# Cross-attention block: norm weights and biases multiplied into the next matrices, three-product values and projection in the first attention, new engine orders

## The reference, cut to what matters

```python
# layer 0
xn = layernorm(x, ln1_w, ln1_b); yn = layernorm(ctx, ln2_w, ln2_b)      # (v - mean) * rstd * w + b
q = xn @ Wq; k, v = split(yn @ Wkv)                                     # 16 heads of 16
x = x + softmax(q k^T / 4) v @ Wproj + bproj
x = x + gelu(layernorm(x, ln3_w, ln3_b) @ W1 + b1) @ W2 + b2            # 256 -> 1024 -> 256
# layer 1
q = rope(rmsnorm(x, norm_w) @ wq); k = rope(ctx @ wkv[k]); v = ctx @ wkv[v]
q, k = q / max(|q|, eps), k / max(|k|, eps)
x = x + softmax(4 q k^T) v @ wout
```

## Time and profile before

| | us |
|---|---|
| median of 3 runs | 366.83 (364.96 to 367.35) |
| the profiled execution, its time | 367.27 |
| its span, first to last instruction | 365.5 |
| PE busy | 357.3 |
| DVE busy | 279.1 |
| ACT busy | 252.7 |
| POOL busy | 193.5 |

### The profile page before, as it was taken

How to read it: one execution, slowest core, us unless ns; L and a number is a source line. 1 busy time by engine, 2 the same in 40 slices (tenths; PEclk the granted TensorE clock), 3 DMA queues, 4 the chain that set the end, 5 groups by cost and what they waited for, 6 DMA issues and landing times.

```text
span 365.5 us, 11432 instructions
## 1 busy us (share of the span) xinstructions
PE 357.3 (98%) x4510; PEld 324.4 (89%) x4510; DVE 279.1 (76%) x654; ACT 252.7 (69%) x490; POOL 193.5 (53%) x194
## 2 busy tenths in 40 slices
PE   8999999999999998999999999999999999999996
PEld 5988888898878887899999999999999999998885
DVE  3699989869598777767886777788877776868752
ACT  2267676676677575774578978976987779966662
POOL 2266433534835338304576458458466755477920
PEclk9999999999999999999999999999999999999999
DMA  7854001100000000000000000000200010000001
...
DMA packets 15724, 12.55 MB, mean 34 GB/s; under 512 B 3252, under 2 KB 15032, under 8 KB 15672
## 3 DMA queue, kind: packets, MB, share of 16 engines
...
## 4 chain that ended last, share of the span: by engine, by line
PE 90%; DVE 6%; issue 2%; ACT 1%; POOL 0%; DVEq 0%; POOLq 0%; ACTq 0%
PE banks_s L1166 12%; PE bank_qk L1046 10%; PE banks_s L1091 7%; PE bank_o L1178 7%; PE bank_y L1178 6%; PE bank_y L1230 4%; PE banks_s L1219 4%; PE bank_t L1126 4%; PE bank_qk L1068 3%; PE bank_y L1147 3%; PE bank_t L1046 3%; PE bank_qk L1072 3%; PE bank_o L1082 3%; DVE row_max L2153 3%; PE bank_o L1210 2%
## 5 line engine op out<-in xcount | busy, mean ns | idle before, releaser
L400 POOL TENSOR_TENSOR norm_inv<-norm_sq_min,minus_half 128x32 f32<-128x32 f32 x16 | 87.6, 5478 | 47.9 <-DVE norm_sq_min L2248 47.9
L354 POOL TENSOR_TENSOR masked<-qkT_r,halves_t 128x512 fp32r<-128x512 f32 x32 | 32.6, 1039 | 60.8 <-DVE qkT_r L2146 60.7
L2153 DVE TENSOR_REDUCE row_max<-banks_s 128x8 f32<-128x1024 f32 x32 | 37.6, 1216 | 2.9 <-PE banks_s L1091 2.5
L575 ACT ACTIVATE PT<-banks_s 128x1024 f32<-128x1024 f32 x32 | 31.1, 1022 | 10.0 <-PE banks_s L1115 9.7
L1166 PE MATMUL banks_s<-lnT_hi,W_hi 128*128 128x256 f32 x120 | 35.4, 295 | 0.0
L676 ACT ACTIVATE PT<-banks_s 128x1024 f32<-128x1024 f32 x32 | 31.5, 1024 | 5.5 <-PE banks_s L1219 5.2
L1166 PE MATMUL banks_s<-lnT_hi,W_lo 128*128 128x256 f32 x120 | 33.9, 282 | 0.0
L1166 PE MATMUL banks_s<-lnT_lo,W_hi 128*128 128x256 f32 x120 | 33.9, 282 | 0.0
L1091 PE MATMUL banks_s<-masked,qkT_r 32*128 32x256 f32 x768 | 31.5, 294 | 0.9 <-DVE row_max L2153 0.7
L1091 PEld LDWEIGHTS banks_s<-masked,qkT_r 32*128 32x128 f32 x768 | 25.0, 183 | 7.5 <-issue 4.7
L619 ACT ACTIVATE W_s<-banks_s,b_cols 128x256 f32<-128x256 f32 x60 | 25.0, 471 | 6.6 <-PE bank_y L1178 4.7
...
## 6 DMA issues: line engine op xcount, KB each, us to landing
...
```

The lines of the kernel that those rows point to most:

```text
L354: nc.gpsimd.tensor_tensor(masked[:, r, 1, :, half, :], qkT_r[:, r, 1, :, :].bitcast(fp32), ones, ALU.mult)\
L400: nc.gpsimd.tensor_tensor(norm_inv[:, j, :], norm_sq_min[:, j, :], minus_half[:, :], ALU.pow).then_inc(c_norm_inv, 1)
L575: nc.scalar.activation(PT[:, 2 * h:2 * h + 2, :], banks_s[:, 2 * h:2 * h + 2, :], ACT.Exp, scale=HD ** -0.5)\
L2153: v.tensor_reduce(row_max[:, 8 * h:8 * h + 8], banks_s[:, 2 * h:2 * h + 2, :].rearrange("p n (r k) -> p (n r) k", k=TOK), AX.X, ALU.max).t ...
```

## The change

1. **Norm weights go into the matrices.** `Wq` is multiplied by `ln1_w` (`query_weight`, ACT), the key half of `Wkv` by `ln2_w` (`keys_weight`, DVE), its value half on the way into high and low parts (`values_weight_hi`, ACT, and `values_weight_lo`, DVE), and `W1` by `ln3_w` in `w1_split`. The biases become products: `ln1_b` with `Wq` gives a column `q_bias`, which `queries_keys_hi` and `queries_keys_lo` add; `ln2_b` with `Wkv` gives a row that is stored in an unused row of the weights, against which `yn` has a column of ones; `ln3_b` with `W1` (`mlp_bias_mm`, 16 float32 products with one column each) is added to `b1`. `centre` and `scale` become `normalise`, one subtraction and multiplication for each input; `centre_b` and `scale_b` become `normalise_b`. The weights and biases arrive by six small DMAs on ACT's queue, one number to a partition, instead of four rows.
2. **`values_a` and `project_a` take the three-product form.** POOL makes the high and low part of the value input (`values_in`, a cast and a subtraction of 128x256), DVE the low part of the projection's input (`on_lo_a`). `queries_keys_hi` is now three ACT instructions instead of one, `queries_keys_lo` three DVE instructions instead of one.
3. **`WARM_LATE` and the two spreading products are gone,** and all engines have new lists. The fillers behind the first `queries_keys_a` are 87 before and 96 after.

A function `head_norms_root`, which would take the power by Newton steps on DVE, is added but never called, as `POWERS` is 16.

```diff
+            def values_in(t):
+                j = t % 2
+                pool.wait_ge(A["inT_ready"], t + 1)
+                wait(pool, A["v_mm"], t - 1)
+                nc.gpsimd.tensor_copy(v_in[:, j, 0, :, :], inT[:, j, 2:4, :]).then_inc(a_v_in_hi, 1)
+                pool.wait_ge(a_v_in_hi, t + 1)
+                nc.gpsimd.tensor_tensor(v_in[:, j, 1, :, :], inT[:, j, 2:4, :], v_in[:, j, 0, :, :].bitcast(fp32), ALU.subtract).then_inc(a_v_in_lo, 1)
...
+                for k in range(KT):
+                    nc.scalar.activation(wq_a[:, k, :], Wq_s[:, k, :], ACT.Copy, scale=ln_cols[:, 0, k:k + 1]).then_inc(wa_q, 1)
...
+            def query_bias():
+                act.wait_ge(q_bias_mm, 1)
+                nc.scalar.activation(q_bias[:, :], bank_qk[:, 0:KT], ACT.Copy).then_inc(q_bias_ready, 1)
+            def context_bias():
+                act.wait_ge(bias_mm, 1)
+                act.wait_ge(c_wkv_padded, 2)
+                nc.scalar.activation(wk_a[C2B:C2B + 1, 1, :], bank_o[C2B:C2B + 1, 0:C1], ACT.Copy).then_inc(k_bias_ready, 1)
+                nc.scalar.activation(wkv_r[C2B:C2B + 1, 0, 1, C1:], bank_o[C2B:C2B + 1, C1:], ACT.Copy).then_inc(v_bias_hi, 1)
+            def out_weight_hi():
+                act.wait_ge(w_out_loaded, 2 * LOADED)
+                nc.scalar.activation(wout_r[:, 0], Wproj_s[:, :, :], ACT.Copy).then_inc(wa_out_hi, 1)
...
                 wait(act, a_shifted, t - 2)
-                nc.scalar.activation(qkT_r[:, t % RING, 0, :, :], bank_qk[:, :].rearrange("p (a b) -> p a b", a=4), ACT.Copy)\
-                    .then_inc(a_qk_hi, 1)
+                for m in range(KT):
+                    nc.scalar.activation(qkT_r[:, r, 0, m, :], bank_qk[:, TOK * m:TOK * m + TOK], ACT.Identity, bias=q_bias[:, m:m + 1])\
+                        .then_inc(a_q_hi, 1)
+                nc.scalar.activation(qkT_r[:, r, 0, KT:, :], by_row(bank_qk[:, 2 * TOK:]), ACT.Copy).then_inc(a_k_hi, 1)
...
+            def query_bias_mm():
+                pe.wait_ge(w_q_loaded, LOADED)
+                for m in range(KT):
+                    for k in range(KT):
+                        last = mm(bank_qk[:, m:m + 1], Wq_s[:, k, 128 * m:128 * m + 128], ln_cols[:, 1, k:k + 1], start=k == 0, stop=k == KT - 1)
+                last.then_inc(q_bias_mm, 1)
+            def context_bias_mm():
+                pe.wait_ge(w_att_loaded, 2 * LOADED)
+                mm(bank_o[:, :], bias_2[:, 0, :], Wkv_s[:, 0, :], start=True, stop=False)
+                mm(bank_o[:, :], bias_2[0:C2B, 1, :], Wkv_s[0:C2B, 1, :], start=False, stop=True).then_inc(bias_mm, 1)
...
-                for k in range(2):
-                    last = mm(bank_o[:, 0:C1], inT[:, t % 2, 2 + k, :], Wkv_s[:, k, C1:], start=k == 0, stop=k == 1)
-                last.then_inc(A["v_mm"], 1)
+                    pe.wait_ge(wa_v_lo, 2)
+                    pe.wait_ge(v_bias_lo, 1)
+                pe.wait_ge(a_v_in_lo, t + 1)
+                split_mm(bank_o[:, 0:C1], v_in[:, t % 2, :, :, :], wkv_r[:, :, :, C1:]).then_inc(A["v_mm"], 1)
...
-                    pe.wait_ge(w_out_loaded, 2 * LOADED)
-                for k in range(KT):
-                    last = mm(bank_y[:, 0:C1], onT[:, k, :], Wproj_s[:, k, :], start=k == 0, stop=k == KT - 1)
-                last.then_inc(A["proj_mm"], 1)
+                    pe.wait_ge(wa_out_lo, 1)
+                pe.wait_ge(a_onT_lo, t + 1)
+                split_mm(bank_y[:, 0:C1], onT_r[:, :, :, :], wout_r[:, :, :, :]).then_inc(A["proj_mm"], 1)
+            def mlp_bias_mm():
+                pe.wait_ge(w1_loaded, LOADED)
+                pe.wait_ge(w_b1_loaded, 4 * LOADED)
+                for m in range(HM):
+                    for k in range(KT):
+                        last = mm(bank_y[:, m:m + 1], W1_s[:, k, 128 * m:128 * m + 128], ln3_cols[:, 1, k:k + 1], start=k == 0, stop=k == KT - 1)
+                last.then_inc(b1_mm, 1)
...
-            for n in range(WARM_EARLY):
+            for n in range(WARM):
                 nc.tensor.transpose(bank_s[n % 4][:, 0:128], ident[:, :], ident[:, :])
-            pe.wait_ge(ln_rows_loaded, 4 * LOADED)
-            pe.wait_ge(ones_ready, 1)
-            mm(bank_qk[:, :], one_row, row_1, start=True, stop=True)
-            mm(bank_o[:, 0:2 * C2], one_row, row_2, start=True, stop=True).then_inc(rows_spread, 1)
-            for n in range(WARM_LATE):
-                nc.tensor.transpose(bank_s[n % 4][:, 0:128], ident[:, :], ident[:, :])
+            pe.wait_ge(ln_rows_loaded, 6 * LOADED)
             pe.wait_ge(bank_zeroed, 1)
-            busy(4, bank_t)
+            busy(7, bank_t)
+            query_bias_mm()
             inputs_a(0)
-            busy(7, bank_o)
+            context_bias_mm()
+            busy(9, bank_y)
+            pe.wait_ge(q_bias_ready, 1)
             queries_keys_a(0)
             pe.wait_ge(A["inT_ready"], 1)
             inputs_a(1)
-            values_a(0)
...
+                    v.tensor_scalar(wk_a[0:r, k, :], Wkv_s[0:r, k, 0:C1], ln_cols[0:r, 2, k:k + 1], None, ALU.mult).then_inc(wa_k, 1)
...
+                v.tensor_scalar(w1_part(W1_hi, u), w1_part(W1_s, u), ln3_cols[:, 0, u % 2:u % 2 + 1], None, ALU.mult).then_inc(w1_hi_done, 1)
                 dve.wait_ge(w1_hi_done, u + 1)
-                v.tensor_tensor(w1_part(W1_lo, u), w1_part(W1_s, u), w1_part(W1_hi, u).bitcast(fp32), ALU.subtract)\
+                v.scalar_tensor_tensor(w1_part(W1_lo, u), w1_part(W1_s, u), ln3_cols[:, 0, u % 2:u % 2 + 1], w1_part(W1_hi, u).bitcast(fp32),
+                                       ALU.mult, ALU.subtract)\
                     .then_inc(w1_lo_done, 1)
...
+            def mlp_bias():
+                dve.wait_ge(b1_mm, 1)
+                v.tensor_tensor(b1_all[:, :], b1_cols[:, :], bank_y[:, 0:HM], ALU.add).then_inc(b1_ready, 1)
...
-            def centre(t):
+            def normalise(t):
...
+                    dve.wait_ge(a_padded, 3)
+                dve.wait_ge(A["rstd_ready"], t + 1)
                 wait(dve, A["in_transposed"], t - 1)
-                v.scalar_tensor_tensor(xn[:, j, :], tile_of(t), mean_var[:, j, 0:1], ln1_rows[:, 0, :],
-                                       ALU.subtract, ALU.mult).then_inc(a_centred, 1)
...
+                v.tensor_scalar(xn[:, j, :], tile_of(t), mean_var[:, j, 0:1], rstd[:, j, 0:1], ALU.subtract, ALU.mult).then_inc(A["norm_done"], 1)
+                v.tensor_scalar(yn[:, j, 0:C2], ctx_in[:, t % AHEAD, 0:C2], mean_var[:, j, 2:3], rstd[:, j, 1:2], ALU.subtract, ALU.mult)\
+                    .then_inc(A["norm_done"], 1)
...
+                dve.wait_ge(a_q_hi, 2 * t + 2)
+                dve.wait_ge(a_k_hi, t + 1)
+                for m in range(KT):
+                    last = v.scalar_tensor_tensor(qkT_r[:, r, 1, m, :], bank_qk[:, TOK * m:TOK * m + TOK], q_bias[:, m:m + 1],
+                                                  qkT_r[:, r, 0, m, :].bitcast(fp32), ALU.add, ALU.subtract)
+                last.then_inc(a_q_lo, 1)
+                v.tensor_tensor(qkT_r[:, r, 1, KT:, :], by_row(bank_qk[:, 2 * TOK:]), qkT_r[:, r, 0, KT:, :].bitcast(fp32),
+                                ALU.subtract).then_inc(a_k_lo, 1)
...
+            def on_lo_a(t):
+                dve.wait_ge(A["onT_ready"], t + 1)
+                v.tensor_tensor(onT_r[:, 1, :, :], by_row(bank_y[:, 0:C1]), onT_r[:, 0, :, :].bitcast(fp32), ALU.subtract)\
+                    .then_inc(a_onT_lo, 1)
```

1448 lines of the change are left out of this document (754 added, 694 removed).

## The result

The changed kernel takes 375.72 us (median of four runs, 374.68 to 376.82) against 366.44 for the kernel before (also four runs, the profiled one among them): ratio 1.0254, 95% interval 1.0222 to 1.0286. It is 9.3 us slower where 3.0 faster was forecast. The kernel before has two groups of executions, 364.0 to 366.1 and 366.8 to 367.5 us, both with a mean granted clock of 0.999 to 1.000, and its profile is of the upper group, so two medians of four runs can differ by 2 us for that alone.

What follows compares the result with a forecast made beforehand. It took PE to bound the kernel (busy 357.3 of 365.5 us), others counting where PE waits. Terms -4.2 + 3.0 - 2.0 + 0.4 - 1.2 + 1.0 = -3.0 from 367.27, less 0.44, gave 363.8 us; range 358.8 to 369.0.

Steps and rivals of the forecast that it cites:

- the start: Kernel start: small DMAs landing at 6.0 us, first queries at 13.5 against 15.48, -2.0 us, ends -3.2 and +0.3.
- the steady stretch: From `shifted_a(1)` to `shifted_a(15)` in the first attention: forecast about -5 us.
- the end: Last part: six fillers ahead of `queries_c(14)` and three POOL powers back to back, +1.0 us, ends 0 and +1.5.
- values and projection term: First attention's `values_a` and `project_a`: three-product form saves 0.14 us a call, 30 calls, -4.2 us, ends -3.0 and -6.3.
- the bias product's cost: `mlp_bias_mm` between `shifted_a(0)` and `shifted_a(1)`: 32 records cost 3.7 us, less 0.7 of removed fillers, +3.0 us.
- the +0.4: From the first queries to `shifted_a(0)`: longer ACT and DVE splits, partly offset by DVE being less behind, +0.4 us.
- the steady first attention: First attention's steady tiles: PE's 2.7 us idle can shrink, 14 added fillers may cost; -1.2 us, ends -2.7 and +1.5.
- these 14 fillers: Fillers behind `shifted_a(0)`, 22 against 8: 1.6 us in all, costing nothing where PE would wait.
- The collision that the forecast mentioned: POOL and DVE share SBUF interfaces: 18 us more POOL work means more hits, each up to 1.0 us of DVE.
- POOL's `v_in`: First attention: PE waits in `values_a` for POOL's value input, mean 0.5 us over 16 tiles, +8.0, 371.8 us; chance 0.12.
- The start gives nothing: Small DMAs land near 8 us or PE stays at lower clock: -1.0 in total, 365.8 to 367 us; chance 0.15.
- The products don't get shorter: Values and projection calls still cost 0.96 us each beside float32 calls: sum +1.2, 368.0 us; chance 0.05.

Runs made afterwards that it cites:

- 64 columns: Changed kernel with the MLP's bias products streaming the bias column 64 times instead of once: 372.73 us; the kernel before with such 64-column products added: 371.24 us.
- the two float32 runs: Changed kernel with 64-column bias products, warm start and reordered DVE list, values and projection as two float32 products again: 373.01 us with fillers, 373.05 without 28 of them.
- the run with less DVE work: Changed kernel with 64-column bias products, warm start, reordered DVE list and no 28 fillers, first attention's residual addition cut to 8 of 256 columns: 369.91 us.
- the other form: Changed kernel with 64-column bias products, warm start and reordered DVE list, one-pass normalisation written as scalar_tensor_tensor instead of tensor_scalar: 369.61 us.

## Why the prediction was wrong

Against the table the forecast misses by 4.0 us at the start, 3.4 between the first two picks, 4.5 in the steady stretch and 0.1 at the end. So three steps failed, about equally. The 4.5 are 0.9 of the values and projection term, 1.0 for a call that moved into the stretch, and 2.6 of waits and fillers.

**The first is the bias product's cost**, "3.7 - 0.7 = +3.0", which priced 32 records at the filler's 0.115 each. The records do cost that while the clock is up: 11 of them start between 38 and 39 us in the changed kernel, and with 64 columns 32 take 3.63 us, 0.113 each. The Trainium skill, "TensorE: Matmul & The Clock Gate", LDWEIGHTS, gives 107 ns for such a load; the trace is 6 ns above. What the sum lacked is that it priced the products at the clock they found. With one column the clock goes to half 2.1 us in; they take 1.3 us more and the calls behind them 1.7 more: 3.0. The rest of the +6.4, 3.4, is the products less the fillers (3.0, as forecast), and 0.4 for a `values_a` call that came in, less waiting that went. The kernel before with the same products added says the same outside the change: +3.5 us with 64 columns, which keep its six fillers, and 1.7 more with one.

**The second is the start**, forecast at -2.0 with "the level rises somewhere inside", and with the +0.4 behind it at -1.6; it came out at +2.4. I wrote that PE waits for six small DMAs and did not ask what the wait does to the clock afterwards. Three profiles whose programs are the same up to there show first queries at 13.97, 16.15 and 17.18; in eleven with filler in the wait they are at 12.4 to 13.2. The sum was wrong besides: the list has nine fillers between `context_bias_mm` and the first queries, 1.0 us at the upper level and 2.0 at the lower, and I counted only ACT's copy, 0.4, in their place. In the five of the eleven where it is earliest `shifted_a(0)` is at 27.9 to 28.2, -1.5 to -1.8. That this is what -2.0 + 0.4 says is partly luck: the first queries are 2.7 to 3.1 earlier than before, and the way from them to `shifted_a(0)` takes 15.4 to 15.7 us instead of 14.2, so +1.2 to +1.5 and not +0.4. The small DMAs landed at 7.4, inside 5 to 8.

**Values and projection**, -4.2: the term is too large by a quarter. 0.11 a call, not 0.14; I had taken 0.96 for float32 from one pair of rows, while the mean of all calls in that trace is 0.92.

**The third is the steady first attention**, -1.2, which came out at +1.4 or so. One more values call stands in the stretch, +0.96 as float32, which the forecast did not count; three products give 2.9 back; from that to the measured -0.5 leaves +1.4. PE's idle in the stretch, which I expected to shrink, is 2.7 us before and 2.8 after, and the fillers, which stand where it would wait, went from 8 to 22, 0.9 to 2.5 us: together 3.6 to 5.3. So the argument "these 14 fillers cost nothing where PE would wait" was right for each filler, and misread as a sign that there is waiting to be saved. Two waits of 1.1 us are most of the 2.8, and one shows its cause:

```profile
129.54 1.31 POOL L383 TENSOR_TENSOR W_lo<-W_s,W_hi 128x512 fp32r<-128x512 f32 x1
129.65 1.32 DVE L2240 TENSOR_SCALAR yn<-ctx_in,mean_var,rstd 128x192 f32<-128x192 f32 x1
131.12 0.41 PE L1127 MATMUL bank_t<-ident,xn 128*128 128x128 f32 x2 [1.08 <-DVE yn L2240]
```

DVE's 192 columns take 0.37 us when POOL is quiet; here they take 1.32, to 0.1 us behind the end of POOL's wide subtraction, and PE stands 1.08 for them. Seven of the 16 are stretched in this way in the changed kernel; in the kernel before the pass over `ctx_in` takes 0.41 us all 16 times. The collision that the forecast mentioned is real and sits on this path. How much of the 1.4 it is in all stays open: the run with less DVE work moved the stretch by 1.1, the other form by nothing.

**The end**, +1.0: measured +1.1, by another sum. The six fillers cost nothing (211.7 us from `shifted_a(15)` to PE's last call with and without them), and the three powers do not follow each other quite; two do, and 16.9 us lie behind them instead of 16.2.

**Rivals.** Slower was given 0.15, on POOL's `v_in`; PE's idle never names it, and POOL had room. "The start gives nothing" met its condition in the profiled execution (first queries at 16.15, at the lower level), but priced it at 365.8 to 367. No rival had a clock that falls again once it is up. "The products don't get shorter" is refuted by the two float32 runs.
